# One step of a 64-step recurrence on VectorE, ScalarE and GpSimd, written another way

## The reference

```python
def step(M, kv):
    k_t, v_t = kv
    v_pred = jnp.einsum('bf,bfd->bd', k_t, M)
    surprise = jnp.linalg.norm(v_t - v_pred, axis=-1, keepdims=True)
    delta = k_t[:, :, None] * v_t[:, None, :]
    M = M + eta_c[None, :, None] * surprise[:, :, None] * delta
    return (_ln2(M), None)
M, _ = jax.lax.scan(step, M0, (kT, vT))
```

## Time and profile before

| | us |
|---|---|
| median of 3 runs | 1951.23 |
| lowest, highest | 1950.62, 1953.53 |
| the profiled execution | 1952.97 |
| its span, first to last instruction | 1951.2 |
| DVE busy, share of the span | 1371.5 (70%) |
| PE busy | 1321.5 (68%) |
| ACT busy | 1150.6 (59%) |
| POOL busy | 977.8 (50%) |

### The profile page before, as it was taken

The page is one execution under the profiler, slowest core; times in us unless marked ns, Lnnn a source line. Parts: engine busy times, 40 slices in busy tenths (PEclk is TensorE's granted clock), DMA queues, the critical chain, the costliest instruction groups (busy, mean ns, idle before and its releaser), DMA issues. The chain is left out here.

```text
span 1951.2 us, 60363 instructions
## 1 busy us (share of the span) xinstructions
PE 1321.5 (68%) x18142; PEld 1074.2 (55%) x18196; DVE 1371.5 (70%) x4938; ACT 1150.6 (59%) x3372; POOL 977.8 (50%) x1502
## 2 busy tenths in 40 slices
PE   6999995988878838995653999200000787849991
PEld 5677773666656628995652777100000565639991
DVE  5899995777787764453555666499999577755575
ACT  4677773777757626774554555365556465526674
POOL 2777775233327757777862444111111454867663
PEclk9999997999989968997886999655555899979995
DMA  2344442311112213333443445200000422223333
GB/s 74 104 113 110 110 113 71 107 50 49 50 43 71 75 51 91 96 92 108 136 135 97 102 88 103 42 1 1 1 1 1 157 66 66 81 64 87 88 114 116
DMA packets 201501, 152.41 MB, mean 78 GB/s; under 512 B 20482, under 2 KB 188802, under 8 KB 200962
## 3 DMA queue, kind: packets, MB, share of 16 engines
q1 hardware_dynamic: 188034, 123.13, 23.9%
q0 software_dynamic: 13312, 27.49, 4.3%
HBM read 76.54 MB, written 65.54 MB: 73 GB/s over the span
## 5 line engine op out<-in xcount | busy, mean ns | idle before, releaser
L1119 PE MATMUL ffn_run_up_ps<-ffn_run_xt,ffn_run_w_now 128*128 128x128 f32 x1792 | 249.4, 284 | 48.9 <-DVE ffn_run_h L1247 20.4
L1089 POOL DMA_INDIRECT expert_outputs<-ffn_run_y_all,ffn_run_ids x224 | 218.8, 977 | 87.1 <-issue 45.8
L1119 PEld LDWEIGHTS ffn_run_up_ps<-ffn_run_xt,ffn_run_w_now 128*128 128x128 f32 x1792 | 224.5, 197 | 61.6 <-ACT ffn_run_xt L1155 31.6
L838 POOL DMA_INDIRECT tokens_by_expert<-ffn_x_all,ffn_dest x192 | 190.7, 993 | 53.2 <-issue 48.8
L1863 PE MATMUL mixer_m_ps<-mixer_mine,mem_state_coef 128*64 128x64 f32 x4 | 0.5, 334 | 283.3 <-DVE mixer_off_in L2000 283.3
L392 POOL TENSOR_TENSOR cross_k_ex<-cross_kt,k_pack 128x256 f32<-128x256 f32 x128 | 76.7, 621 | 197.8 <-ACT cross_kt L591 197.6
L1128 PE MATMUL ffn_run_y_ps<-ffn_weights,ffn_run_h 128*128 x1216 | 173.1, 276 | 0.7 <-DVE ffn_run_y_all L1264 0.5
L1595 POOL TENSOR_TENSOR recur_rho<-recur_var_eps_new,k_pack 128x1 f32<-128x1 f32 x64 | 34.9, 545 | 247.5 <-DVE recur_var_eps_new L1689 247.5
L1863 PEld LDWEIGHTS mixer_m_ps<-mixer_mine,mem_state_coef 128*64 128x64 f32 x4 | 0.3, 206 | 283.4 <-DVE mixer_ones L1998 283.4
L1128 PEld LDWEIGHTS ffn_run_y_ps<-ffn_weights,ffn_run_h 128*128 128x128 f32 x1216 | 154.5, 193 | 1.1 <-issue 1.1
L1156 ACT COPY ffn_run_w_now<-ffn_weights 128x512 f32 x224 | 139.5, 623 | 0.0
(11 more groups left out here) (337 smaller groups left out, 4685.1 us busy)
## 6 DMA issues: line engine op xcount, KB each, us to landing
ffn_run_x<-tokens_by_expert SPq DMA_DIRECT2D x56, 260.0 KB, 3.0
tokens_by_expert<-fill_zeros SPq DMA_DIRECT2D x32, 292.5 KB, 2.8
ffn_run_yg<-expert_outputs SPq DMA_DIRECT2D x16, 512.0 KB, 4.9
memory_rows<-products_row SPq DMA_DIRECT2D x16, 390.0 KB, 4.6
ffn_weights<-memory_rows SPq DMA_DIRECT2D x16, 390.0 KB
tokens_by_expert<-fill_zeros SPq DMA_DIRECT2D x32, 162.5 KB, 2.6
ffn_weights<-in_pack_ffn SPq DMA_DIRECT2D x1, 4112.0 KB, 14.6
self_turned<-in_x_turned SPq DMA_DIRECT2D x64, 64.0 KB, 1.8
```

The costliest lines, as they stand in the source:

```text
L838: pool.indirect_dma_start(xs[h], bass.IndirectOffsetOnAxis(ap=self.dest[:, r, t:t + 1], axis=0), self.x_all[:, t, :], None)\
L1089: pool.indirect_dma_start(ys, bass.IndirectOffsetOnAxis(ap=ids[:, t:t + 1], axis=0), y_all[:, t, :], None)\
L1119: mm = nc.tensor.matmul(up_ps[t.slot(2)][:, c * P:(c + 1) * P], w_now[:, t.slot(2), c * P:(c + 1) * P], xt[:, t.slot(2), :], start=True, s ...
```

## The change

The three programs of the recurrence are rewritten; the stage ahead puts the column of sums first in each block instead of last (column 0, tokens in 1 to 64).

- The offset becomes column 0 of a tensor `state` [128, 65], with the weights in columns 1 to 64. One product `row` then holds the offset's part too, the scaling by `rho` covers it, and `off`, `gg`, `pm` and their instructions are gone.
- The large product moves to GpSimd (`parts`, two buffers). It is made for step t+1 out of `cv`, which VectorE now writes early in step t (L1671). The sum along rows stays on VectorE (L1677) and needs GpSimd's `sums_ready`.
- The variance before the eps is 1 - eps x rho^2 after each step, so ScalarE keeps `var_eps` with one instruction; it takes the standard deviation `sigma` as a second square root (L1615), and VectorE makes `rho` by a reciprocal (L1697). GpSimd's power is gone.
- The update of `quad` is written as a polynomial in c_t: z = square x c_t + past, quad = z x c_t + quad_kept. `square` comes from ScalarE a step ahead (L1617), `past` out of `common` (L1684), `quad_kept` is quad x rho^2 (L1702).

```diff
 # memory_products
-                            lhs, rhs = ((kt[:, s2, rows], ket[:, s2, b, :]), (vt[:, s2, b, 0:S], vt[:, s2, b, :]),
-                                        (ket[:, s2, b, 0:S], ket[:, s2, b, :]))[n]
+                            lhs, rhs = ((kt[:, s2, rows], ket[:, s2, b, :]), (vt[:, s2, b, 1:S + 1], vt[:, s2, b, :]),
+                                        (ket[:, s2, b, 1:S + 1], ket[:, s2, b, :]))[n]
...
 # memory_recurrence, GpSimd
-            for t in range(S):
-                pool.wait_ge(root_asked, 2 * t + 2)
-                pool.tensor_tensor(v["rho"], v["var_eps_new"], k["half"][:, 0:1], ALU.pow).then_inc(root_ready, 1)
+            for t in range(S - 2):
+                n, rest = t + 1, S - 2 - t
+                pool.wait_ge(weights_ready, t + 1)
+                if t > 1:
+                    pool.wait_ge(common_ready, t - 1)
+                pool.tensor_tensor(parts[:, (t + 1) % 2, 0:rest * n].rearrange("p (a b) -> p a b", b=n), g[:, later(t), KK + 1:KK + 1 + n],
+                                   cv[:, t % 2, 0:n].unsqueeze(1).to_broadcast([P, rest, n]), ALU.mult).then_inc(sums_ready, 1)
 # ScalarE
+            act.activation(v_len[:, :], flat[:, VV + 1:VV + 1 + (S - 1) * (ROW + 1) + 1:ROW + 1], ACT.Sqrt).then_inc(squares, 1)
...
             for t in range(S):
+                act.wait_ge(root_asked, t + 1)
+                act.activation(state[:, t + 1:t + 2], v["r2c"], ACT.Sqrt, bias=g[:, t, VV + 1 + t:VV + 2 + t]).then_inc(root_ready, 1)
+                if t:
+                    act.wait_ge(kept, 2 * t - 1)
+                    act.activation(v["var_eps"], v["rho2"], ACT.Identity, scale=-LN_EPS, bias=v["one_eps"]).then_inc(kept, 1)
...
+                act.activation(v["sigma"], v["h2"], ACT.Sqrt, scale=state[:, t + 1:t + 2], bias=v["var_eps"]).then_inc(root_ready, 1)
+                if t < S - 2:
+                    act.activation(square[:, (t + 1) % 2, later(t)], g[:, later(t), KK + 2 + t], ACT.Square,
+                                   scale=v_len[:, t + 1:t + 2]).then_inc(squares, 1)
+                if t < S - 1:
+                    act.wait_ge(inverse_ready, t + 1)
+                    act.mul(v["rho2"], v["rho"], v["rho"]).then_inc(kept, 1)
 # VectorE, one step
+                stt(out=v["h2"], in0=c_t, scalar=dd[:, col], in1=v["cross2"], op0=ALU.mult, op1=ALU.add).then_inc(h2_ready, 1)
+                need(last_scaled)
+                moved = put(stt(out=state[:, 0:1], in0=p_n[:, col], scalar=c_t, in1=state[:, 0:1], op0=ALU.mult, op1=ALU.add))
...
+                stt(out=cv[:, t % 2, 0:nx], in0=state[:, 1:nx + 1], scalar=2.0, in1=g[:, nx, VV + 1:VV + 1 + nx],
+                    op0=ALU.mult, op1=ALU.mult).then_inc(weights_ready, 1)
+                need(moved)
+                row_ready = put(tt(row[:, 0:nx + 1], state[:, 0:nx + 1], g[:, nx, KK:KK + nx + 1], ALU.mult))
+                if t:
+                    dve.wait_ge(sums_ready, t)
+                    dve.tensor_reduce(common[:, rest], parts[:, t % 2, 0:(S - nx) * t].rearrange("p (a b) -> p a b", b=t), AX,
+                                      ALU.add).then_inc(common_ready, 1)
+                need(row_ready)
+                h = put(ttr(out=junk[:, 1, 0:nx + 1], in0=row[:, 0:nx + 1], in1=sv2[:, 0:nx + 1], scale=1.0, scalar=0.0,
+                            op0=ALU.mult, op1=ALU.add, accum_out=v["h"]))
+                if t:
+                    dve.wait_ge(common_ready, t)
+                    past_ready = put(stt(out=past[:, rest], in0=common[:, rest], scalar=v["rho"], in1=g[:, rest, KK + nx],
+                                         op0=ALU.mult, op1=ALU.mult))
...
+                z_ready = put(stt(out=z[:, rest], in0=square[:, t % 2, rest], scalar=c_t, in1=past[:, rest], op0=ALU.mult, op1=ALU.add))
+                kv = put(ttr(out=junk[:, 2, 0:nx + 1], in0=row[:, 0:nx + 1], in1=g[:, nx, VV:VV + nx + 1], scale=-2.0, scalar=0.0,
+                             op0=ALU.mult, op1=ALU.add, accum_out=v["kv_neg2"]))
+                need(z_ready)
+                quad_ready = put(stt(out=quad[:, rest], in0=z[:, rest], scalar=c_t, in1=quad_kept[:, rest], op0=ALU.mult, op1=ALU.add))
...
+                dve.reciprocal(v["rho"], v["sigma"]).then_inc(inverse_ready, 1)
+                need(h, quad_ready)
+                mm = put(stt(out=v["mm"], in0=row[:, 0:1], scalar=v["h"], in1=quad[:, ncol], op0=ALU.mult, op1=ALU.add))
...
+                    kept_quad = put(ts(quad_kept[:, far], quad[:, far], v["rho"], v["rho"], ALU.mult, ALU.mult))
+                need(mm, kv)
+                u = put(stt(out=v["u"], in0=v["mm"], scalar=v["rho"], in1=v["kv_neg2"], op0=ALU.mult, op1=ALU.add))
+                last_scaled = put(ts(state[:, 0:nx + 1], state[:, 0:nx + 1], v["rho"], None, ALU.mult))
+                need(u)
+                ts(v["r2c"], v["u"], v["rho"], vv_neg[:, ncol], ALU.mult, ALU.max).then_inc(root_asked, 1)
...
```

More of the change, by code:

```diff
@@ L1576, in memory_recurrence @@
         g = room[:, 0:S * ROW].rearrange("p (t r) -> p t r", r=ROW)
-        prod = sb("prod", [P, S * S // 4])
-        junk = sb("junk", [P, 3, S])
-        quad = sb("quad", [P, S])
+        flat = g[:, :, :].rearrange("p t r -> p (t r)")
+        parts = sb("parts", [P, 2, S * S // 4])
+        junk = sb("junk", [P, 3, S + 1])
+        quad, quad_kept, z, past = (sb(n, [P, S]) for n in ("quad", "quad_kept", "z", "past"))
+        square = sb("square", [P, 2, S])
         common = sb("common", [P, S])
-        cv, row, wt, half_gain, gain = (sb(n, [P, S]) for n in ("cv", "row", "wt", "half_gain", "gain"))
@@ L1662, in _ @@
[L1662 to L1663 removed]
+            put(dve.memset(quad_kept[:, :], 0.0))
+            put(dve.memset(past[:, :], 0.0))
+            put(dve.memset(state[:, 0:1], 0.0))
+            put(dve.memset(v["one_eps"], 1.0 + LN_EPS))
+            put(dve.memset(v["cross2"], 0.0))
+            need(put(dve.memset(v["var_eps"], LN_EPS)))
+            dve.memset(junk[:, 0, :], 0.0).then_inc(prepared, 1)
+            cross_ready = last_scaled = done[0]
@@ L1737, in _ @@
+                cross_ready = put(ttr(out=junk[:, 0, 0:nx + 1], in0=state[:, 0:nx + 1], in1=g[:, nx, PP:PP + nx + 1], scale=2.0 / N_MEM,
+                                      scalar=0.0, op0=ALU.mult, op1=ALU.add, accum_out=v["cross2"]))
             dve.wait_ge(root_ready, 2 * S)
-            dve.wait_ge(new_terms, 2 * S - 1)
-            dve.wait_ge(offsets, 3 * S - 2)
-            need(put(ts(coef[:, :], coef[:, :], v["rho"], None, ALU.mult)))
-            put(ts(offset, v["off_new"], v["rho"], None, ALU.mult))
+            need(put(dve.reciprocal(v["rho"], v["sigma"])))
```

144 lines of the change are left out of this document (38 added, 106 removed).

## The result

| | before | after |
|---|---|---|
| median of 20 runs each, side by side, us | 1949.22 | 1952.91 |
| lowest, highest | 1942.97, 1953.53 | 1949.03, 1957.33 |
| the profiled execution | 1952.97 | 1954.95 |
| its span | 1951.2 | 1953.2 |
| 63 steps, first `h2` to the last | 255.8 | 259.7 |

The change makes the kernel slower by a ratio of 1.0021, with a 95% interval of 1.0012 to 1.0030, some 4 us. The forecast was 8.7 us faster. What was to be gained on VectorE's chain was gained, and a little more than that was given back at one dot product.

The account below looks back on a forecast made before the run. VectorE's chain was taken to bound the recurrence: 255.8 us would become 223.7 + 24.8 = 248.5, a gain of 7.3, with 1.4 from set-up and end 8.7, so 1942.5 us. Range 1914 to 1970, the forecast's own 1936 to 1950.

Parts of the forecast that it names:

- What bounds the kernel: Recurrence: VectorE's chain sets its time, 255.8 us for 63 steps; a microsecond off the chain is one off the kernel.
- The new step on VectorE: Rewritten chain without a hold: middle step from 4.66 to 3.85 us, mean 3.55, 63 steps 223.7 us, a gain of 32.1.
- Costs hidden: Recurrence step: second root `sigma` is ready long before VectorE asks; reciprocal taken at its cheap end, 0.21 us, costing nothing.
- Set-up and end: Both ends of the recurrence: 1.2 us off ahead of the first `h2`, 0.2 off the end, together 1.4.
- The door: GpSimd's product holds VectorE's two-input dot product `h` behind the sum to its end: 0.4 us a step, 24.8 us.
- Rival 2: No door for two-input VectorE instructions: the full gain of 33.5 us stands, 1917.7 us; chance 22%.
- I take 1.67: GpSimd's large product: price of 1.67 ns an element, so 1.31 us for the mean product of 672 elements.
- rival 1: Same door, but GpSimd's product at 2.12 ns an element: held 0.72 us a step, 11.1 us slower, 1962.3 us; chance 30%.
- turning point: Sum of gain and hold: the sign turns at a delay of 0.54 us a step, about 1.85 ns an element.
- The hold of 24.8 us: Dot product `h` behind the sum: held by GpSimd's product 0.4 us a step over 62 steps, 24.8 us.
- Rival 3: GpSimd is the bound: above about 3.3 ns an element the next sum waits, 20 us or more slower, 1972 upwards; chance 6%.

Follow-up runs that it names:

- one row only: Against the change, GpSimd multiplies one row of the large product and the rest reads as zero: 1915.53 us, ratio 0.9829 to the kernel before.
- The kernel with the fills: Against the change, two GpSimd fills of the product's size, which write and read nothing, replace the product: 1913.31 us, steps 220.7 us.
- the one with the dot products first: Against the change, both dot products with `row` stand ahead of the sum, directly behind `row`: 2016.34 us, steps 321.4 us.

## Why the prediction was wrong, and where it was right

**What bounds the kernel** was right: in every kernel above the span of the profiled execution less the steps' sum lies between 1689 and 1695 us, while the sum goes from 220.7 to 321.4.

**The new step on VectorE** was right: 3.85 us reckoned for the middle and 3.84 measured with the long product away, 3.55 and 3.50 in the mean, 223.7 and 220.7 for the 63 steps. Of the 3 us, 1.9 are the rounding up from 3.52 to 3.55.

**Costs hidden** was right. `sigma` ends 0.72 behind `h2` (1379.90 + 0.39 against 1379.57), and VectorE asks for it far later: the reciprocal starts 2.47 behind it where nothing is held (1357.19 to 1359.66 with one row only), for 2.54 reckoned. The reciprocal takes 156 ns, less than either of its bounds (0.21 and 0.27), and VectorE is nowhere idle before it or before `quad_kept`. One load of ScalarE's table serves the whole stretch. Set-up and end gave 1.46 us for 1.4.

**The door** was right: the held instruction is the one named, L1680, and it ends 0.05 us behind GpSimd at 32 columns, as taken. The kernel with the fills and the one with the dot products first make it more exact: GpSimd's writing doesn't close it, which leaves the reading, and it is closed for the whole product. By the Trainium skill's rule ("SBUF — State Buffer", Who interferes with whom), which excepts GpSimd instructions that only write and VectorE instructions with one SBUF input outside the 2-port modes, the runs agree in both exceptions: 184 ns beside fills, and 846 ns for the sum beside the product against 841 alone. One input alone doesn't free an instruction: the one that the earlier trace rows shows held in the mixer, a TENSOR_SCALAR, has one tensor as input. Rival 2, which denied the door, falls.

**The step that failed** is "I take 1.67". The product costs 0.19 us and 1.95 ns an element over the range of sizes: (2.12 - 0.31) us over 992 - 62 elements, from the largest row above and from the one of step 1,

```profile
1250.49 0.31 POOL L1597 TENSOR_TENSOR recur_parts<-ffn_weights,recur_cv 128x62 f32<-128x62 f32 x1 [24.60 <-DVE recur_cv L1671]
```

The forms of 1.67 were chosen because they multiply and because one operand is repeated, as here. The first is no reason (addition 1507 ns, multiplication 1508). The second looked at the wrong axis: in those forms the repeated operand stays on one value along the inner axis, here it runs through n values there and is repeated over rows outside. With the operand on one value the same product takes 1.68 ns an element (and at 4 columns and below, or in a single row, it makes no difference). The prediction had written down this very difference, as the ground for rival 1, and chose the cheap price all the same.

The sum was that near to its turning point, 1.85 ns, that this one choice made the sign. With 1.95 in the prediction's own working the mean product ends at 0.52 + 0.19 + 1.31 = 2.02, the dot product at 2.07 instead of 1.46: 0.61 a step, 37.8 us in place of 24.8 (39.0 measured). Then 223.7 + 37.8 - 255.8 - 1.4 = 4.3 us slower. Measured were 0.21%, 4.1 us. This agreement is luck in part: term by term the profiles give 220.7 + 39.0 - 255.8 - 1.9 = 2.0 us slower, which is what the two profiled executions differ by, and the chain put too long makes up for the hold put too short.

The hold of 24.8 us was short by 14.2. Of these the price makes 39.0 - 27.5 = 11.5, by the kernel with one value. The other 2.7 were missing even for the cheap product, 1.2 of them in rounding 0.42 us a step to 0.4.

**Rival 1** had the right cause and sign, with a price too high: 2.12 from one row of one size, with the fixed part borrowed from other forms. A row that lies 0.02 us above the line (459 ns, where 0.19 + 1.95 x 128 = 0.44 us) becomes 0.17 ns an element when it is divided by 128 elements, and that was most of the difference between 11 us slower and 4. The estimate of 2.1 that was worked out from the Trainium skill ("GPSIMD Engine Reference", Performance versus the Vector engine) lies 8% above the measured 1.95. Why the addition of 128 elements stands above the line is open; it was not tried.

**Rival 3**, GpSimd as the bound, falls: the largest product ends 0.53 + 2.12 = 2.65 us behind `h2`, over 2 us ahead of the sum that asks for it (1380.06, 5.25 behind that `h2`), and the sum's idle time is 0.0. The 3.5 us that the prediction gave the product are those of the mean step; by its own starts the largest has 3.84, so this rival needed 3.7 ns an element, not 3.3.

## What to carry to other kernels

Work moved to GpSimd beside VectorE is free only as far as VectorE has work to do over it that it isn't held at, here a sum with one input; its first two-input instruction behind that waits for GpSimd's end, and in the profile this looks like a long busy instruction, not like idle time. Look for an instruction whose mean is several times that of its twin. Undo a move alone before judging a rewriting: the rewritten step was worth 8.0 us, and the move to GpSimd took 11.9 back. When both engines have a cover that is too short, divide the work: here all on GpSimd cost 39.0 us, all on VectorE 27.1, and 53% on GpSimd 7.3. And a price per element is to be taken from a form whose operands run along the inner axis in the same way, at two sizes.
